# Transfers placed between the scatters, one-hot rows moved to VectorE, and two sums taken another way, in a Fourier-feature attention and expert-routing kernel

## The reference

```python
q, k, v = (x @ W.T + b for each of q, k, v)      # 16 heads of 8 numbers
p  = einsum('blhd,dm->blhm', q or k, proj_mat) / sqrt(8)
q', k' = concat([cos(p), sin(p)]) / sqrt(128)    # 256 features per head
kv  = einsum('blhm,blhd->bhmd', k', v)
out = einsum('blhm,bhmd->blhd', q', kv) @ Wo.T + bo
x = layernorm(x + out)
route_w = softmax(x @ Wr + br); keep the 2 largest of 8 experts, renormalised
x = layernorm(x + sum over kept experts of w * (relu(x @ W1 + b1) @ W2 + b2))
```

## Time and profile before

| | us |
|---|---|
| three runs, median | 550.03 (547.97 to 550.23) |
| the profiled execution, its own time | 551.36 |
| its span | 549.6 |
| PE busy | 483.9 (88%) |
| DVE busy | 427.8 (78%) |
| POOL busy | 410.7 (75%) |
| ACT busy | 381.0 (69%) |

### The profile page before, as it was taken

One profiled execution on the slowest core, in us unless ns is written; L12 is line 12 of the kernel. 1 busy time (PEld: TensorE's weight loads), 2 busy tenths in 40 slices (PEclk: granted clock), 3 DMA queues, 4 the chain that ended last, 5 costly groups with the idle time before them and its releaser, 6 DMA issues.

```text
span 549.6 us, 13153 instructions
## 1 busy us (share of the span) xinstructions
PE 483.9 (88%) x4205; PEld 297.4 (54%) x4205; DVE 427.8 (78%) x907; ACT 381.0 (69%) x533; POOL 410.7 (75%) x474
## 2 busy tenths in 40 slices
PE   6698889999999999999999989689999679999914
PEld 3333344444444444444344444158999678999802
DVE  6769978988988988988988888568677475777654
ACT  2686669789789789789789689376555244565325
POOL 2279549879879889879879889857677656777645
PEclk9899989999999999999999999799999789999957
DMA  4675504705704705604605400032222123222174
GB/s 96 169 228 160 127 1 138 195 16 144 203 20 126 206 17 144 190 16 141 153 15 136 126 17 1 8 84 58 69 65 71 59 75 94 70 65 70 39 273 191
DMA packets 44447, 56.03 MB, mean 102 GB/s; under 512 B 8779, under 2 KB 31541, under 8 KB 44381
## 3 DMA queue, kind: packets, MB, share of 16 engines
q1 hardware_dynamic: 39493, 45.86, 30.5%
q0 software_dynamic: 4320, 8.95, 5.0%
q10 hardware_dynamic: 568, 0.38, 0.2%
HBM read 37.22 MB, written 17.94 MB: 100 GB/s over the span
## 4 chain that ended last, share of the span: by engine, by line
PE 55%; POOL 12%; DVE 12%; issue 9%; ACT 6%; DMA 2%; another core or an unknown queue 2%; SPq 1%; DVEq 0%; ACTq 0%; POOLq 0%
PE ang L786 11%; PE ang L795 10%; PE misc L603 7%; PE ang L583 5%; PE misc L638 5%; DVE turns L1067 5%; DVE feats L1075 4%; POOL feats L1430 3%; PE ang L574 3%; PE ang L570 3%; POOL routed_dram L1561 2%; PE misc L512 2%; PE misc L649 2%; ACT rows_s L893 2%
## 5 line engine op out<-in xcount | busy, mean ns | idle before, releaser
L1067 DVE TENSOR_SCALAR turns<-ang 128x1024 f16<-128x1024 f32 x128 | 155.4, 1217 | 46.4 <-PE ang L574 23.4
L873 ACT ACTIVATE feats<-ang 128x1024 f32<-128x1024 f32 x128 | 131.7, 1029 | 63.6 <-PE ang L583 61.1
L1430 POOL TENSOR_TENSOR feats<-feats 128x1024 f32<-128x1024 f32 x56 | 107.0, 1910 | 48.8 <-ACT feats L874 48.4
L874 ACT ACTIVATE feats<-ang 128x1024 f32<-128x1024 f32 x128 | 131.5, 1028 | 0.0
L1075 DVE TENSOR_TENSOR feats<-feats 128x1024 f32<-128x1024 f32 x72 | 102.5, 1423 | 0.7 <-ACT feats L874 0.6
L1591 POOL DMA_INDIRECT expert_dram<-feats x71 | 69.7, 981 | 36.3 <-DVE feats L1354 28.5
L1561 POOL DMA_INDIRECT routed_dram<-rows_s,slots x64 | 76.3, 1193 | 20.7 <-issue 18.3
L583 PE MATMUL ang<-turns,negi 128*128 128x512 f16 x256 | 77.9, 386 | 12.4 <-DVE turns L1067 10.5
L795 PE MATMUL ang<-experts,feats 128*128 x568 | 77.6, 281 | 5.5 <-DVE feats L1314 5.4
L786 PE MATMUL ang<-feats 128*128 128x128 f32 x568 | 78.1, 282 | 4.5 <-DVE feats L1306 2.2
L944 ACT ACTIVATE feats<-experts 128x644 f32 x71 | 52.5, 739 | 36.8 <-DVE feats L1354 25.3
(11 more groups left out here) (195 smaller groups left out, 597.2 us busy)
## 6 DMA issues: line engine op xcount, KB each, us to landing
stk<-parts_dram SPq DMA_DIRECT2D x189, 96.0 KB
parts_dram<-parts SPq DMA_DIRECT2D x16, 384.0 KB, 3.6
feats<-routed_dram SPq DMA_DIRECT2D x72, 65.5 KB
feats<-expert_dram SPq DMA_DIRECT2D x16, 256.0 KB, 5.4
x_all<-attn_x SPq DMA_DIRECT2D x8, 256.0 KB, 4.8
experts<-ffn_W SPq DMA_DIRECT2D x8, 256.0 KB
out<-feats SPq DMA_DIRECT2D x8, 256.0 KB, 2.2
x_in<-attn_x SPq DMA_DIRECT2D x7, 256.0 KB
```

What stands on the lines that cost most here:

```text
L873: act.activation(f[:, 0, :], a, ACT.Sin, scale=TWO_PI)
L874: act.activation(f[:, 1, :], a, ACT.Sin, scale=TWO_PI / 2).then_inc(s["sines"], 1)
L1067: dve.tensor_scalar(turns[:, u % 2, :], ang[:, slot(ph, u), :], MAGIC, -MAGIC, ALU.add, ALU.add)\
L1430: pool.tensor_tensor(f, f, f, ALU.mult).then_inc(s["sq_p"], 1)
```

## The change

1. **SP's order.** A batch's q-side reads were issued a batch ahead. Now they go out in units 4 to 7 of the batch itself, one group of heads a unit, each (but the first) followed by one expert load. The k-side reads of the next batch go out around units 9 to 13. W1 is loaded one expert at a time.
2. **One-hot rows.** POOL's cast, two subtractions and compare go away. DVE makes the rows with two `is_equal` instructions on the indices themselves, in unit 11 behind the copy L1079. POOL fills the `meta` columns first, then waits for the one-hot rows and adds them.
3. **Split.** On POOL the cast becomes a second subtraction from the same f32 value, written as bf16, ahead of the subtraction in place. The first batch's split on DVE stays.
4. **Sum of v.** DVE's copy of x^T also gives the sum of x over the tokens (an accumulator output). `kv_turn` takes one matmul of this sum, broadcast, with a scaled Wv in place of the four, and the bias part is added in `kv_evac`, whose two copies become additions. Three set-up instructions on DVE prepare the operands in unit 1 of the first batch; the memset of `minus_2` goes.

```diff
+        def split_apart(eng, b, side):
+
+            wait(eng, "kq"[side] + "_ev", 1, b, 1)
+            f = qk_f[:, side, :]
+            p = parts[:, side, :, :]
+            n = 3 * side
+            eng.tensor_tensor(p[:, 1, :], f, p[:, 0, :], ALU.subtract).then_inc(s["split"], 1)
+            wait(eng, "split", 6, b, n + 1)
+            eng.tensor_tensor(f, f, p[:, 0, :], ALU.subtract).then_inc(s["split"], 1)
+            wait(eng, "split", 6, b, n + 2)
+            eng.tensor_tensor(p[:, 2, :], f, p[:, 1, :], ALU.subtract).then_inc(s["split"], 1)
...
+            def second_side(b):
+
+                for hg in range(HG):
+                    at_unit(b, READS_AT + hg)
+                    read(b, 1, hg)
+                    if hg and b < BATCH - 1:
+                        load_expert(3 * (b - 1) + hg - 1)
+
+            def next_batch(b):
+
+                write(b, 0)
+                read(b, 0, 0)
+                read(b, 0, 1)
+                write(b, 1)
+                for hg in range(2, HG):
+                    at_unit(b - 1, 10 + hg)
+                    read(b, 0, hg)
+
+            for b in range(1, BATCH):
+                if b > 1:
+                    second_side(b - 1)
+                if b < BATCH - 1:
+                    load_x(b + 1)
+                next_batch(b)
+            second_side(BATCH - 1)
...
                 pe.matmul(o[:, P:2 * P], kvT[:, 1, :], ident4[:, :], start=True, stop=False, skip_group_check=True)
-                for t in range(LT):
-                    mm = pe.matmul(o[:, P:2 * P], minus_2[:, :], dense(v_pad[:, t, :, :]),
-                                   start=False, stop=(t == LT - 1), skip_group_check=True)
-                mm.then_inc(s["kv_mm"], 1)
+                pe.matmul(o[:, P:2 * P], x_sum[:, b % 2, :].broadcast_to([P, P]), wv_sum,
+                          start=False, stop=True, skip_group_check=True).then_inc(s["kv_mm"], 1)
...
-                dve.tensor_copy(xT[:, :], misc[:, 0, :]).then_inc(s["xT_ev"], 1)
+                dve.tensor_scalar(xT[:, :], misc[:, 0, :], 1.0, None, ALU.mult, ALU.add,
+                                  accum_out=x_sum[:, b % 2, :]).then_inc(s["xT_ev"], 1)
...
-                dve.tensor_copy(kv_c[:, :], misc[:, 0, P:2 * P])
-                dve.tensor_copy(dense(kv_pad[:, :, :, :].rearrange("p a g w -> p (a g) w")),
-                                misc[:, 0, 0:2 * P].rearrange("p (g a d) -> p g a d", a=HG, d=DH))\
+                dve.tensor_tensor(kv_c[:, :], misc[:, 0, P:2 * P], bv_sum[:, 1, :], ALU.add)
+                dve.tensor_tensor(dense(kv_pad[:, :, :, :].rearrange("p a g w -> p (a g) w")),
+                                  misc[:, 0, 0:2 * P].rearrange("p (g a d) -> p g a d", a=HG, d=DH),
+                                  bv_sum[:, :, :].rearrange("p k (g a d) -> p (k g) a d", a=HG, d=DH), ALU.add)\
...
+            def one_hot(b):
+
+                hold(dve, "idx_ok", 1, b, 1)
+                for k in range(TOPK):
+                    ins = dve.tensor_tensor(hot[:, k, :, :], over(iota[:, :].unsqueeze(1), tile8),
+                                            over(idx8[:, :, k:k + 1], tile8), ALU.is_equal)
+                ins.then_inc(s["hot_ok"], 1)
...
-            AFTER_ROUND = ((5, residual), (10, largest))
+            AFTER_ROUND = ((5, residual), (10, largest), (11, one_hot))
...
+                        dve.memset(bv_sum[:, 0, :], 0.0)
+                        dve.tensor_scalar(bv_sum[:, 1, :], bv_bc[:, 0, :], -2.0 * LEN, None, ALU.mult)
+                        dve.wait_ge(s["raw_ev"], 2)
+                        dve.tensor_scalar(wv_sum, wT[:, 2, :], -2.0 * KV_SCALE, None, ALU.mult)\
+                            .then_inc(s["vs_ok"], 1)
...
                     if u in (7, 9) and not last:
-                        split(pool, b + 1, (u - 7) // 2)
+                        split_apart(pool, b + 1, (u - 7) // 2)
...
                 hold(pool, "idx_ok", 1, b, 1)
-                pool.tensor_copy(pick_no[:, :, :], idx8[:, :, 0:TOPK]).then_inc(s["no_ok"], 1)
-                wait(pool, "no_ok", 1, b, 1)
-                for k in range(TOPK):
-                    ins = pool.tensor_tensor(hot[:, k, :, :], over(iota[:, :].unsqueeze(1), tile8),
-                                             over(pick_no[:, :, k:k + 1], tile8), ALU.subtract)
-                ins.then_inc(s["off_ok"], 1)
-                hold(pool, "off_ok", 1, b, 1)
-                pool.tensor_scalar(hot[:, :, :, :], hot[:, :, :, :], 0.0, None, ALU.is_equal).then_inc(s["hot_ok"], 1)
+                pool.tensor_tensor(rows_s[:, :, P + 2:XW], top8[:, :, 0:1], top8[:, :, 1:2], ALU.subtract)
+                pool.tensor_copy(rows_s[:, :, P:P + 1], idx8[:, :, 0:1])
+                pool.tensor_scalar(rows_s[:, :, P + 1:P + 2], rows_s[:, :, P + 1:P + 2], float(LEN), None, ALU.add)\
+                    .then_inc(s["meta"], 1)
                 wait(pool, "hot_ok", 1, b, 1)
                 pool.tensor_tensor(picks[:, :], hot[:, 0, :, :].rearrange("p t e -> p (t e)"),
                                    hot[:, 1, :, :].rearrange("p t e -> p (t e)"), ALU.add).then_inc(s["picked"], 1)
```

More of the change, by code:

```diff
@@ L77 @@
 SENDS_AT = 27
+READS_AT = 4
 SUMS_ON_PE = (4, 6, 7)
@@ L243, in build @@
             "angles", "rounded", "reduced", "sines", "sq_v", "sq_p",
[L245 removed]
+            "xT_mm", "xT_ev", "vs_ok", "q_mm", "q_ev", "k_mm", "k_ev", "v_mm", "v_ev", "split", "parts_out",
             "kvT_mm", "kvT_ev", "kv_mm", "kv_ev", "c_mm", "c_ev", "out_mm", "out_ev", "wo_mm",
             "y_ok", "bo_ok", "ln_stat", "ln_aggr", "ln_eps", "ln_pow", "ln_shift", "xn_ok", "xr_mm", "xr_ev",
[L251 removed]
+            "lg_mm", "lg_ok", "top_ok", "idx_ok", "hot_ok", "picked", "meta", "rk_mm", "slot_ok", "based",
             "slotk_ok", "slots_ok", "scattered", "pads_at", "pads_in", "rt", "tab_ok",
@@ L379, in _, with write, read, at_unit @@
                 sp.dma_start(dst, src).then_inc(s["late_in"], 16)
[L381 to L404, removed]
+            def write(b, side):
+                hold(sp, "split", 6, b, 3 * side + 3)
+                dst = parts_dram[b, side].rearrange("i r n -> r i n")
+                sp.dma_start(dst, parts[:, side, :, :]).then_inc(s["parts_out"], 16)
+                hold(sp, "parts_out", 32, b, 16 * side + 16)
+            def read(b, side, hg):
+                hold(sp, "angles", UNITS, b, HALF * side + 2 * hg + 2 - UNITS)
+                rows = parts_dram[b, side].rearrange("i (d h) n -> (i d) (h n)", d=DH)
+                src = rows[:, hg * G * LEN:(hg + 1) * G * LEN]
+                for j in range(SPL):
+                    sp.dma_start(stk[j * SPL * DH:(j + 1) * SPL * DH, side, hg, :, :].rearrange("p g n -> p (g n)"),
+                                 src).then_inc(stk_in[side][hg], 16)
+            def at_unit(b, u):
+                hold(sp, "angles", UNITS, b, u + 1)
             def load_x(b):
@@ L411, in _ @@
             load_x(1)
-            stack(0)
+            for side in range(2):
+                write(0, side)
+                for hg in range(HG):
+                    if side or hg:
+                        read(0, side, hg)
             for t in range(BATCH):
@@ L1296, in _ @@
             square(e, -1)
-            LAST_PIECES = ((1, residual), (2, statistics), (3, moments), (16, take_logits), (17, largest), (18, which),
+            LAST_PIECES = ((1, residual), (2, statistics), (3, moments), (16, take_logits), (17, largest), (18, which), (19, one_hot),
                            (23, take_ranks), (24, move_base), (26, slot_numbers))
```

36 lines of the change are left out of this document (13 added, 23 removed).

## The result

The changed kernel took 564.78 us (median of four, 561.74 to 567.76), the kernel before beside it 550.13 (547.97 to 553.44): a ratio of 1.029, 95% interval 1.023 to 1.035. The forecast was 556.0 with a range up to 560.5; the side was right, the size was not. Later executions showed that the answer depends on the chip: on some chips the kernel before takes 537 us and the change costs 0.7%, on others, that of this comparison among them, it takes 550 and the change costs 2.9%. (One of those later executions of the changed kernel took 1592 us; the ratios leave it out.)

What follows compares the result with a forecast made beforehand. PE looked busiest (39.31 of 41.0 us a batch), but DVE was taken to arrive last at unit 13. 4.1 + 0.6 + 1.9 - 0.6 = +6.0 on the profiled 551.36 gave 557.4, or 556.0 for the median; range 548.5 to 560.5.

Steps and rivals of the forecast that it cites:

- the price of the change in the scatters' stretch: Around POOL's scatters: later reads judged harmless, a shorter scatter only lengthening POOL's wait for ACT; taken as 0.
- a scatter or load effect: Rival, slower: more collisions in the first batch's tail or ranks after DVE's slot sum, +10, 560.0; chance 0.10.
- the delay at unit 13: Steady batch, PE's q' product waiting for DVE: 0.15 + 0.35 + 0.18 = 0.68 us later, six times, +4.1.
- Its chain of causes: Units 11 to 13: POOL's longer split delays a DVE square, then POOL's square, which holds the one-hot pair 0.35.
- the slack of 0.1 for the picks: Steady batch: ranks ready at 178.3, before DVE's slot sum at 178.4; its loss covered by the upper bound.
- PE's new gap of over 1 us: Sign to look for: in a steady batch PE stands over 1 us ahead of L638 in unit 13.
- the copy of x^T: DVE's copy with accumulator output: 0.09 us more a batch, seven times, +0.6 (0 to 1.1).
- the first batch, +1.9: Set-up instructions put DVE's square behind POOL's in the first batch, delaying PE: +1.9 us (0.4 to 2.2).
- the last batch, -0.6: Picks 0.8 sooner, less 0.2 for a DVE one-hot instruction: -0.6 (-1.5 to 0); PE's wait about 3.9.
- SP's order, 0: New order of reads and loads: q-side reads leave units 4 to 7, used from unit 8; cost 0.
- PE was not the bound: Rival, faster: PE sets the pace, so fewer matmuls in unit 13 win 6.4 us, 543.6; chance 0.15.
- Only instructions: Rival, same: one-hot pair finds ports free, first squares keep their order; +1.5, 551.5; chance 0.23.

Runs made afterwards that it cites:

- e_hot: Kernel before with only the one-hot pair on DVE and the shorter choosing on POOL, on a chip of 550 us: ratio 1.058.
- a_again: The changed kernel, unchanged, run again on a chip of 537 us: ratio 1.007, period 41.58 us.
- b_sum: Kernel before with only the sum of v taken from the running sum of x, on 537 us: ratio 0.998, period 41.05 us.
- b_order: Kernel before with only SP's new order of loads, on 537 us: ratio 1.000, period 41.04 us.
- d_sum: Kernel before with only the new sum of v, the same program as b_sum, on a chip of 550 us: ratio 0.998.
- a_split_back: The changed kernel with the old split (subtract, cast, subtract) of k and q, on 537 us: ratio 1.001 to the kernel before.
- a_q_back: The changed kernel with the old split for q alone, on 537 us: ratio 1.000 to the kernel before.
- a_hot_back: The changed kernel with the old choosing on POOL and no one-hot rows on DVE, on 537 us: ratio 1.025 to the kernel before.

## Why the prediction was wrong

**The step that failed** is the price of the change in the scatters' stretch, from unit 14 to unit 2 of the next batch, which the sum took as 0. It speaks of that stretch only under SP's order ("POOL waits 1.77 for ACT after them ... I take 0"), and it prices the one-hot rows where they stand, in units 11 to 13, and nowhere behind. In place of this 0 PE's results come 1.1 to 1.2 late in four batches and 5.38 in the last, 9.2 us more than before, and a spell of the clock at half rate follows the long one. By e_hot the one-hot part is enough to bring such stalls; why it does stays open. The kernel before has one such wait in its batches (0.75 in the chain) and 7.4 us of them in the expert phase. The prediction did not ask what these were, nor keep room for more. The rival "a scatter or load effect" had the right side and a name that fits, but its means (more collisions in the first batch, late ranks) are not what came: that it is the nearest is luck. It had 0.10 of the chance.

**Without the stalls** the forecast stands better: a ratio of 1.007 on 537 is +3.8 us (+1.6 to +5.9) against +6.0. By its terms:
- the delay at unit 13, forecast 0.68 (0.18 to 1.0). From the copy of kvT on, where 0.53 of the 0.68 lie, it is 0.79 by the rows above, of which the pair takes 0.65; the period of a_again is 0.53 longer. Its chain of causes (split, DVE square, POOL square, one-hot pair) was seen at each step, and taking back q's split alone removes most of it;
- the slack of 0.1 for the picks was not there: PE waits 1.05 for them. DVE still arrives last (PE's next wait, 0.27, is for the base), so it cost little. So PE's new gap of over 1 us, foretold ahead of unit 13's product, came in two pieces, the larger in unit 12 and for POOL;
- the copy of x^T, forecast 0.09 a batch: 0.01. The rounding follows it at 0.61; the accumulator's own row, 0.08 to 0.09 long, lies inside the copy's tail. (The Trainium skill, VectorE: DVE Perf Modes, "Two Vector instructions with no wait between them", counts two instructions: right, and the second is nearly free.) b_sum's period is b_order's;
- the first batch, +1.9: up to the first copy of kvT it came in two of the three profiled executions of the changed kernel (+1.8 and +2.2), not in the first (+0.25), where POOL's square was late by 0.03. In all three it was followed by -2.2, and in all three the clock stayed up at 70. The prediction had no term for the clock. This one is not the change's own either: b_sum and d_sum, one program, have 46.9 and 48.5 there, without and with the fall of the clock;
- the last batch, -0.6: from the start of `chosen` to the ranks it was 1.58, forecast 0.8, measured 0.81 (359.54 to 360.35). The ranks come 6.25 behind the copy of kvT (354.10), before it was 6.77: 0.5 won. But PE's wait, forecast 3.9, did not shrink, since PE itself, with less of `kv_turn`, begins to wait earlier;

```profile
360.35 0.21 PE L702 MATMUL misc<-picks,tri 128*128 128x32 f16 x1 [4.68 <-POOL picks L1580]
```

- SP's order, 0: right twice on chips of 537 (1.0001, and 1.0067 beside 1.0070), not tried on those of 550.

**The rivals.** PE was not the bound: with a quarter of `kv_turn`'s sums it stands and waits, and b_sum, where they are gone from the kernel before, is at 0.998. "Only instructions" (+1.5) is near what a_split_back and a_q_back, with less of the change, come to: 1.001 and 1.000.

## What to carry to other kernels

Two engines that exclude each other make the price of an instruction a matter of who comes 0.02 us earlier; so work out for a moved instruction what the other engine starts just ahead of it, and what becomes late behind it, in both orders. A pause of PE can cost twice, since the clock may fall behind it: give every new wait of the size seen here (1.0 to 1.8 us) that possibility in the range. And read what the chain cannot name ("unknown queue") as a cost that the change can multiply, and leave room for it; one chip's ratio need not be another's.

## What was not expected of the hardware

- The same program and kernel before run at 537 or at 550 us by the chip, and a change of a few small instructions at 0.997 or 1.058. In the two profiled executions of the changed kernel at 550 the stalls return in place and length: they end at 149.22 and 151.17, each 15.5 us behind its copy of kvT, after 1.16 and 1.19; 5.38 and 5.41 in the last batch. In the three of the kernel with the pair and the sum most take 4.7 to 4.8 or 5.7 us and end 19.2 to 19.4 behind the copy of kvT, but which batches have which, or none, changes from execution to execution. What makes PE's results late there stays open. The loading of instructions does not fit, since its transfers drift against the batches (in the changed kernel one comes at 149.2, beside the stall of 148.06, and none of that queue between 269.3 and 284.4, around the stall of 277.40). The order of the loads does not decide it, since d_sum and e_hot both have the old one and only e_hot stalls in its batches.
- The two kinds of chip differ in the expert phase as well: b_sum and d_sum, one program, take 195.6 and 204.0 us from the last copy of kvT to the end, and only 4.0 of the 8.4 stand in the chain as stalls.
- TensorE's clock falls now and then behind a wait of 1.0 to 1.8 us: in one of the middle batches of a_again, in four periods of seven in a_hot_back, at a cost of 1.4 to 1.7 us each time.
